# Two layers of a transformer block on one core: the shared expert cut as 384 + 320 units, with the last 64 of up and of gate in one tile

## The reference

```python
x = x + xattn(layernorm(x), ctx)            # 4 x 512 tokens, width 512, context width 256
h = rmsnorm(layernorm(x)); x2 = layernorm(x) + attention(h)      # 16 heads of 128, causal
t = rmsnorm(x2).reshape(2048, 512)
probs = softmax(t @ gate_w.T)               # 16 experts, the 6 best of each token, shares scaled to 1
routed = sum over the six: share * (silu(t @ eg.T) * (t @ eu.T)) @ ed.T      # 352 units an expert
shared = (silu(t @ sg_w.T) * (t @ su_w.T)) @ sd_w.T                          # 704 units, all 2048 tokens
out = x + x2 + routed + shared
```

## Time and profile before

| what | value |
|---|---|
| median of three runs | 2272.8 us |
| the profiled execution | 2274.86 us |
| its span, first to last instruction | 2273.0 us |
| mean granted TensorE clock | 0.979 |
| TensorE matmul busy | 2154.1 us, 95% |
| VectorE, ScalarE, GpSimd busy | 51%, 31%, 43% |
| `shared_expert`, first to last matmul | 1243.7 to 1482 us |

### The profile page before, as it was taken

One profiled execution on the slowest core, in us unless ns is written; L12 is line 12 of the kernel. 1 busy time (PEld: TensorE's weight loads), 2 busy tenths in 40 slices (PEclk: granted clock), 3 DMA queues, 4 the chain that ended last, 5 costly groups with the idle time before them and its releaser, 6 DMA issues. The chain is left out here.

```text
span 2273.0 us, 39678 instructions
## 1 busy us (share of the span) xinstructions
PE 2154.1 (95%) x11914; PEld 1870.6 (82%) x11915; DVE 1159.6 (51%) x2531; ACT 710.2 (31%) x1831; POOL 966.3 (43%) x1025
## 2 busy tenths in 40 slices
PE   6879999999999999999996999979999999999997
PEld 5668888989888898888875767779999999999996
DVE  5745646464655646465666576623333333333342
ACT  5633434343433434343434111012222222222221
POOL 1225454553645454553605035424444444444443
PEclk9989999999999999999998999989999999999998
DMA  3113344343434344343416111076776676667443
GB/s 134 61 47 112 126 153 138 123 172 120 139 124 152 112 159 154 111 168 114 158 38 245 43 65 46 33 248 157 189 196 156 179 200 162 157 182 201 83 78 56
DMA packets 139827, 300.64 MB, mean 132 GB/s; under 512 B 16704, under 2 KB 16704, under 8 KB 137472
## 3 DMA queue, kind: packets, MB, share of 16 engines
q1 hardware_dynamic: 114528, 241.25, 30.1%
q0 software_dynamic: 24960, 58.21, 13.5%
q10 hardware_dynamic: 288, 0.53, 0.1%
HBM read 177.51 MB, written 122.42 MB: 132 GB/s over the span
## 5 line engine op out<-in xcount | busy, mean ns | idle before, releaser
L567 POOL TENSOR_TENSOR chunk_hi<-chunk_raw,zero 128x512 fp32r<-128x512 f32 x153 | 159.3, 1041 | 242.2 <-DMA chunk_raw<-in_whole 242.2
L1575 DVE TENSOR_TENSOR prod<-ps,silu 128x352 f32<-128x352 f32 x111 | 58.2, 525 | 313.2 <-PE ps L62 274.4
L569 POOL TENSOR_TENSOR chunk_raw<-chunk_raw,chunk_hi 128x512 fp32r<-128x512 f32 x153 | 197.7, 1292 | 12.0
L785 DVE TENSOR_TENSOR pT_lo<-ps,pT_hi 128x384 fp32r<-128x384 f32 (+2 forms) x256 | 111.1, 455 | 176.5 <-ACT pT_hi L726 172.6
L1425 POOL DMA_INDIRECT out<-y,sidx x111 | 176.6, 1591 | 55.9 <-issue 35.1
L1432 POOL TENSOR_TENSOR carry<-ident 128x1 f32<-128x1 f32 x218 | 41.1, 188 | 327.1 <-DVE gidx L1572 256.7
L757 DVE SCALAR_TENSOR_TENSOR HS<-ps,rinv,HS 128x512 f32<-128x512 f32 x260 | 176.6, 738 | 2.8 <-PE ps L62 2.8
L715 ACT ACTIVATE prob<-ps,negmax 128x512 f32<-128x512 f32 (+3 forms) x256 | 131.6, 527 | 110.0 <-DVE negmax L746 110.0
L60 PE MATMUL ps<-wv_or_qk_hi,hT_hi 128*128 128x256 f32 x512 | 146.2, 286 | 8.3 <-POOL wv_or_qk_lo L562 8.3
L60 PE MATMUL ps<-ring,xT_0hi 128*128 x448 | 150.5, 336 | 1.7 <-DMA ring<-split_weights 1.7
L60 PE MATMUL ps<-ring,hT_hi 128*128 x333 | 140.8, 423 | 10.7 <-issue 9.0
(11 more groups left out here) (298 smaller groups left out, 6100.2 us busy)
## 6 DMA issues: line engine op xcount, KB each, us to landing
ring<-split_weights SPq DMA_DIRECT2D x240, 272.0 KB
chunk_raw<-in_whole SPq DMA_DIRECT2D x153, 256.0 KB, 2.6
split_weights<-chunk_hi SPq DMA_DIRECT2D x153, 256.0 KB, 2.4
split_weights<-chunk_raw SPq DMA_DIRECT2D x153, 256.0 KB, 2.6
xg<-in_wqk SPq DMA_DIRECT2D x16, 512.0 KB, 3.6
x<-in_x SPq DMA_DIRECT2D x4, 1024.0 KB, 5.6
xg<-in_wv SPq DMA_DIRECT2D x8, 512.0 KB, 4.0
x_spill<-x SPq DMA_DIRECT2D x4, 1024.0 KB, 3.9
```

The costliest lines, as they stand in the source:

```text
L567: nc.gpsimd.tensor_tensor(chunk_hi[k][:], chunk_raw[k][:], zero[:].to_broadcast([P, CH]), ALU.add).then_inc(chunk_high, 1)
L569: nc.gpsimd.tensor_tensor(chunk_raw[k][:].bitcast(F32R), chunk_raw[k][:], chunk_hi[k][:].bitcast(F32), ALU.subtract).then_inc(chunk_low, 1)
L785: nc.vector.tensor_tensor(pT[1][:, 0:split, w], ps_t[k % 2][:, 0:split * P].rearrange("p (j t) -> p j t", t=P), pT[0][:, 0:split, w].bitca ...
```

## The change

The 704 units are cut as 384 + 320. The first half has three full chunks of 128. The second has two full chunks and one last tile: in its 128 weight columns stand the last 64 units of up (columns 0 to 63) and the last 64 of gate (columns 64 to 127). So its 12 matmuls give up in partitions 0 to 63 and gate in 64 to 127 of one bank of `ps_u`. ScalarE takes silu of partitions 64 to 127 and writes it to partitions 0 to 63. In n = 4 to 7 the silu of the last chunk waits for pe_u, since there is no gate bank for it.

For down, that chunk's high part lies in partitions 0 to 63 and its low part in partitions 64 to 127 of one tile, and the high part of the down weights lies there twice. One matmul over 128 partitions gives high by high and low by high together; a second over 64 partitions gives high by low. So the chunk takes two matmuls a tile and not three.

The host lays the weights out to match; `warm` is loaded with 3072 columns a part instead of 2816, `wgu_1` with 2560 instead of 2816. The size of all of them together and of the space they lie in is unchanged, and so are all steps n = 0 to 3 but for the width of their third chunk (128 units instead of 96). The table work and its slots are unchanged.

```diff
+SHARED = [3 * P, 2 * P]
+REST = NSH * I - sum(SHARED)
+SGU = [2 * DC * SHARED[0], 2 * DC * SHARED[1] + DC * P]
+SAT = [0, SGU[0] + DN]
-WARM = EW + GU
+WARM = EW + SGU[0]
...
             for half in range(2):
-                sp.dma_start(warm[:, half * EW:half * EW + GU].bitcast(F32), split_w[half][:, 0:GU]).then_inc(ld_w, 16)
+                sp.dma_start(warm[:, half * EW:half * EW + SGU[0]].bitcast(F32), split_w[half][:, 0:SGU[0]]).then_inc(ld_w, 16)
...
+        w_rest = [w[:, 2 * DC * SHARED[1]:SGU[1]].rearrange("p (c i) -> p c i", c=DC) for w in wgu_1]
+        rest = lambda n, c: n >= NBLK and c == NI - 1
...
-                    for c, (_, w) in enumerate(IT):
-                        last = matmul3(nc, ps_d[i % 2][:], [h[0:w, c, i * P:(i + 1) * P] for h in hh[n % 2]],
-                                       [x[0:w, c, :] for x in wdn_s], c == 0, c == NI - 1)
+                    for c in range(NI):
+                        h_hi, h_lo = [h[:, c, i * P:(i + 1) * P] for h in hh[n % 2]]
+                        w_hi, w_lo = [x[:, c, :] for x in wdn_s]
+                        if rest(n, c):
+                            nc.tensor.matmul(ps_d[i % 2][:], h_hi, w_hi, start=False, stop=False)
+                            last = nc.tensor.matmul(ps_d[i % 2][:], h_hi[0:REST], w_lo[0:REST], start=False, stop=True)
+                        else:
+                            last = matmul3(nc, ps_d[i % 2][:], (h_hi, h_lo), (w_hi, w_lo), c == 0, c == NI - 1)
...
+                    if rest(n, c):
+                        for j in range(DC):
+                            h_hi, h_lo = [h[:, j, blk * S:(blk + 1) * S] for h in hT]
+                            w_hi, w_lo = [x[:, j, :] for x in w_rest]
+                            bank = ps_u[q % 2]
+                            nc.tensor.matmul(bank[:], w_hi, h_hi, start=j == 0, stop=False)
+                            nc.tensor.matmul(bank[:], w_hi, h_lo, start=False, stop=False)
+                            last = nc.tensor.matmul(bank[:], w_lo, h_hi, start=False, stop=j == DC - 1)
+                        last.then_inc(pe_u, 1)
+                        into_table(n, c)
+                        continue
...
-                    act.wait_ge(pe_g, q + 1)
+                    if rest(n, c):
+                        act.wait_ge(pe_u, q + 1)
+                    else:
+                        act.wait_ge(pe_g, q + 1 - max(0, n - NBLK))
...
-                    nc.scalar.activation(silu[0:w, :], ps_g[q % 2][0:w, :], ACT.Silu).then_inc(act_s, 1)
+                    if rest(n, c):
+                        nc.scalar.activation(silu[0:REST, :], ps_u[q % 2][REST:P, :], ACT.Silu).then_inc(act_s, 1)
+                    else:
+                        nc.scalar.activation(silu[:], ps_g[q % 2][:], ACT.Silu).then_inc(act_s, 1)
...
-                    nc.vector.tensor_tensor(hh[n % 2][1][0:w, c, :], prod[0:w, :],
-                                            hh[n % 2][0][0:w, c, :].bitcast(F32), ALU.subtract).then_inc(dve_h, 1)
+                    low = hh[n % 2][0][REST:P, c, :] if rest(n, c) else hh[n % 2][1][:, c, :]
+                    nc.vector.tensor_tensor(low, prod[0:w, :], hh[n % 2][0][0:w, c, :].bitcast(F32), ALU.subtract).then_inc(dve_h, 1)
```

More of the change, by code:

```diff
@@ L43 @@
 EW = GU + DN
-WARM = EW + GU
+SGU = [2 * DC * SHARED[0], 2 * DC * SHARED[1] + DC * P]
+SAT = [0, SGU[0] + DN]
+WARM = EW + SGU[0]
+assert SAT[1] + SGU[1] + DN == NSH * EW and WARM + 2 * SGU[1] <= EW + 3 * GU
 SLOTS = 3
@@ L990, in shared_expert @@
         at = placing(nc, slab + 4 * WARM)
-        gate_up = lambda w: w.rearrange("p (m c i) -> p m c i", m=2, c=DC)
-        wgu_1 = [at(f"wgu_1{s}", [P, GU], F32R) for s in ("hi", "lo")]
-        wgu_s = [[gate_up(warm[:, half * EW:half * EW + GU]) for half in range(2)], [gate_up(w[:]) for w in wgu_1]]
+        gate_up = lambda w, k: w[:, 0:2 * DC * SHARED[k]].rearrange("p (m c i) -> p m c i", m=2, c=DC)
+        wgu_1 = [at(f"wgu_1{s}", [P, SGU[1]], F32R) for s in ("hi", "lo")]
+        wgu_s = [[gate_up(warm[:, half * EW:half * EW + SGU[0]], 0) for half in range(2)], [gate_up(w[:], 1) for w in wgu_1]]
+        w_rest = [w[:, 2 * DC * SHARED[1]:SGU[1]].rearrange("p (c i) -> p c i", c=DC) for w in wgu_1]
+        rest = lambda n, c: n >= NBLK and c == NI - 1
         wdn_s = [sb(f"wdn_{s}", [P, NI, D], F32R) for s in ("hi", "lo")]
@@ L1053, in load_down @@
                     sp.dma_start(wdn_s[half][:].rearrange("p c n -> p (c n)").bitcast(F32),
-                                 split_w[half][:, k * EW + GU:(k + 1) * EW]).then_inc(ld_dn, 16)
+                                 split_w[half][:, SAT[k] + SGU[k]:SAT[k] + SGU[k] + DN]).then_inc(ld_dn, 16)
             def load_ring(half, columns):
@@ L1062, in _ @@
             for half in range(2):
-                sp.dma_start(wgu_1[half][:].bitcast(F32), split_w[half][:, EW:EW + GU]).then_inc(ld_gu, 16)
+                sp.dma_start(wgu_1[half][:].bitcast(F32), split_w[half][:, SAT[1]:SAT[1] + SGU[1]]).then_inc(ld_gu, 16)
             sp.wait_ge(pe_u, NI * NBLK)
@@ L1144, in _ @@
                     pe.wait_ge(ld_gu, 32)
-                for c, (i0, w) in enumerate(IT):
+                for c in range(NI):
                     q = NI * n + c
@@ L1148, in _ @@
                         pe.wait_ge(dve_p, q - 1)
+                    if rest(n, c):
[9 more added lines that the diff above has]
+                        continue
+                    i0 = c * P
                     for m, bank in enumerate((ps_g[q % 2], ps_u[q % 2])):
                         for j in range(DC):
-                            last = matmul3(nc, bank[0:w, :], [x[:, m, j, i0:i0 + w] for x in wgu_s[k]],
+                            last = matmul3(nc, bank[:], [x[:, m, j, i0:i0 + P] for x in wgu_s[k]],
                                            [h[:, j, blk * S:(blk + 1) * S] for h in hT], j == 0, j == DC - 1)
@@ L1310, in _ @@
             for n in range(STEPS):
-                for c, (_, w) in enumerate(IT):
+                for c in range(NI):
+                    w = REST if rest(n, c) else P
                     q = NI * n + c
@@ L1660 @@
     whole = np.concatenate([gu, down.reshape(NE, len(IT), P, D).transpose(2, 0, 1, 3).reshape(P, NE, DN)], axis=2)
-    whole = np.concatenate([whole[:, E:NE], whole[:, 0:E]], axis=1).reshape(P, NE * EW)
+    sg, su = (chunks(w(k).T) for k in ("sg_w", "su_w"))
+    sd = w("sd_w").T
+    half = lambda lo, hi: [m[:, :, lo:hi].reshape(P, -1) for m in (sg, su)]
+    rows_of = lambda lo, hi: chunks(sd[lo:hi]).reshape(P, -1)
+    ends = slice(NSH * I - REST, NSH * I)
+    shared = np.concatenate([*half(0, SHARED[0]), rows_of(0, SHARED[0]), *half(SHARED[0], sum(SHARED)),
+                             np.concatenate([su[:, :, ends], sg[:, :, ends]], axis=2).reshape(P, -1),
+                             rows_of(SHARED[0], sum(SHARED)), np.concatenate([sd[ends], sd[ends]])], axis=1)
+    whole = np.concatenate([shared, whole[:, 0:E].reshape(P, E * EW)], axis=1)
     whole = np.concatenate([whole, np.zeros((P, (CHUNKS + 2) * CH - NE * EW), np.float32)], axis=1)
```

10 lines of the change are left out of this document (6 added, 4 removed).

## The result

The changed kernel takes 2263.7 us (median of six runs, 2261.79 to 2265.53), the kernel before 2272.61 (six runs, 2270.62 to 2276.34). The ratio is 0.996 with a 95% interval of 0.9947 to 0.9973, so 8.9 us less, the interval 6 to 12. The profiled execution has a span of 2261.8 us against 2273.0.

What follows compares the result with a forecast made beforehand. TensorE's matmuls bound the kernel (95% busy), except short slots, paced by the table makers' round trip. Merged chunks 8.56 us plus slot (7, 6) 0.23 gave 8.8 off at the DMA queue: median 2272.8 to 2264.0 us, range 2259 to 2268.5.

Steps and rivals of the forecast that it cites:

- The pace of the short slots: Down's slots ending with a table: GpSimd's round trip sets the period, 3.23 to 3.26 us; one matmul less wins nothing.
- The naive 14.8 us: Steps 4 to 7: 64 matmuls less at 0.232 us, if nothing else sets the pace; as a rival 8%.
- The merged chunk: Last chunk of steps 4 to 7: 12 matmuls less gain 2.14 us a step, 8.56 in four, not 2.78 a step.
- silu for the most part: Steps 4 to 7: most of the 0.64 us lost a step is silu without its cover, the rest in_column.
- "0.232 us each, whatever the width", and steps 0 to 3 at nothing: Gate and up matmuls start 0.232 us apart at any width; a third chunk of 128 units in steps 0 to 3 costs nothing.
- The matmul over 64 partitions at 0.232: Down, steps 4 to 7: priced like 96 and 128 partitions; slot (7, 6) gains 0.23 us, down(7) 0.93.
- The drain rival: Down: the 64-partition matmul and the next wait for an empty array, 0.16 us each, twice a slot; 2264.6 us; 15%.
- The DMA queue sets the stage's end: Stage's end: a backlog from the third block's store ends the stage 8.8 us earlier; without backlog 9.7.
- the sign given for it: Stage's end: last add to the padding's landing takes longer than before by up to 0.9 us.
- Loads ahead of the stage: Before the stage: `warm` grows by 0.26 MB, 0.6 us; the norm behind it lands later but is covered, costing nothing.
- The slower rival: Steps 4 to 7: TensorE's idling lowers the granted clock to 1.2 GHz, matmuls 0.43 us apart, up to 2312 us; 5%.
- Given back in GpSimd: Shorter slots: three in_lane go from 2.45 to 3.88 us beside VectorE; all gains 2.1, 2270.7 us; rival, 12%.

Runs made afterwards that it cites:

- e2: The changed kernel with down's second product over all 128 partitions and issued twice, so nine matmuls a tile again: 2263.02 us, one run.
- e8: Against e6, the same 32 table batches spread over the step, after gate, after up and after two tiles of down: 2244.15 us, ratio 0.9869.
- e1: The changed kernel with the second product of down's last chunk over all 128 partitions instead of 64: 2262.81 us, ratio 0.9946.
- e10: The kernel before, nothing merged, with its table batches spread after gate and up of each chunk and once in down: 2259.06 us, ratio 0.993.
- e3: The changed kernel with the merged chunk's silu reading the gate bank of the chunk before, waiting for nothing new: 2258.91 us, one run.
- e4: The kernel before with only the shared expert's gate and up weights laid out chunk by chunk: 2269.73 us against 2275.26, ratio 0.9979.
- e7: Against e1, the third block of finished rows stored in four tiles, each after its own add: 2263.44 us, ratio 0.9957.
- e9: Against e8, the third block stored in tiles and the ring's remaining load issued before them: 2242.22 us, ratio 0.9864.
- e6: Against e1, the merged chunk as first instead of last in steps 4 to 7: 2260.84 us, ratio 0.9946.

## Why the prediction was right, point by point

The forecast of 2264.0 us came out at 2263.7, inside 2259 to 2268.5, and faster. The main mechanism was right and was shown, but that the medians agree to 0.3 us is in part luck: the interval of the difference is 6 to 12 us, and the profiled stage became 9.67 us shorter, not 8.8. Two terms were wrong. At TensorE's end they went against each other; at the stage's end only the first counts, since the queue begins to fill before most of the second.

- **The pace of the short slots**: right. Periods in down 3.23 to 3.26 us, unchanged (e2), and gone when the tables are moved (e8). The wait there is 0.44 us and not the 0.64 laid out; the 64-partition matmul has used up the difference (e1 has 0.65). The naive 14.8 us would have been the change's worth only with the tables elsewhere (e10).
- **The merged chunk**: 4.17 us was laid out for the first period, 4.18 measured; 3.86 for the second, 3.92 measured. The sum of 2.14 us a step was 2.07 (10.17 less 8.10). What was said of its parts was wrong: not silu for the most part, but silu and in_column side by side, with 0.13 us for silu alone (e3).
- **"0.232 us each, whatever the width", and steps 0 to 3 at nothing**: wrong on the gain's side. The distance went from 0.232 to 0.227 in the chunks not merged, a layout effect (e4): slot (5, 1) took 5.98 us instead of 6.10 and (5, 0) 6.10 instead of 6.22. The six such slots from (5, 0) to (7, 1) give 0.7 us, and table (4, 1) came 0.39 us earlier after the stage's start; but the time up to it differs by 0.7 us between two profiles of the same changed kernel (113.47 and 112.77), so that part is within its own spread.
- **The matmul over 64 partitions at 0.232**: wrong on the other side. The drain rival, given 15%, had the mechanism right. It put 0.16 us on each side, 0.32 a tile; measured are 0.09 before it, 0.20 after it and 0.10 one matmul later, 0.39. In the slots with a table it is hidden; in slot (7, 6) and in down(7) it took more than the 0.23 that a matmul less should give: from table (7, 5) to the last add the changed kernel needs 11.74 us, the kernel before 11.13. So TensorE's and VectorE's end came 8.68 us earlier after the stage's start (229.63 against 238.31), not 9.72.
- **The DMA queue sets the stage's end**: right, shown by e1, where TensorE ended 1.85 us earlier and the stage did not. But the sign given for it did not come: the way from the last add to the next stage was to grow by up to 0.9 us, and it shrank from 5.43 to 4.44, since the add came later and the queue earlier than laid out. The queue began to fill 9.30 us earlier (out stored at 1464.44 and 1474.50, less the stages' starts), not 8.79, and the stage ended 9.67 earlier, not 8.8. The 9.67 add up from the merged chunks' 8.2, the layout's 0.7, the 0.39 up to table (4, 1) and 0.37 in the queue behind the store. Tiles alone took 0.76 us off the way from the last add to the next stage (e7 against e1), tiles and an earlier load of the ring 2.05 (e9 against e8).
- **Loads ahead of the stage**: the norm of the third group started at 1216.98 after 0.21 us of idle, and ScalarE's copies of it at 1225.72, 8.7 us later (8.2 before). The norm was not late, and it was covered, as said.
- **The clock**: 1.00 throughout steps 4 to 7. The slower rival did not come.
- **Given back in GpSimd**: three in_lane took 2.01 to 2.45 us before and 2.01 to 2.32 after. It did not come either.

The Trainium skill (TensorEngine Tiling (Array Packing), Key Properties) says that changing the tiling mode drains TensorE. The trace of the changed kernel agrees: 0.32 and 0.43 us around the 64-partition matmul and 0.33 behind them, where 0.23 stands in e1.

## What to carry to other kernels

Before pricing matmuls taken away, look at what ends the wait behind them: with a second work woven in at fixed places, its round trip (here 3.26 us) is a floor for each slot. The same work at evenly spaced places took 17 us off the stage of the changed kernel (e6 to e8) and 15 off that of the kernel before (e10), where the arithmetic saved had given 9.7. Where two late inputs meet, price the step without each of them in turn; what each "costs" is not a share of the whole. And a product over half of the partitions among products over all of them was not cheaper but dearer (e1): fill the other half with something harmless, if the operands stand there anyway.

## What the runs showed of the hardware that was not expected

- A matmul over 64 partitions among matmuls over 128 costs 0.39 us more than its own 0.23: 0.09 before it, with its weight load late by 0.35, 0.20 after it and 0.10 one matmul later. 96 partitions among 128 cost nothing (0.23).
- The same matmuls, counts and shapes come 0.227 or 0.232 us apart by the place of their weight tiles in SBUF: 5.98 against 6.10 us for 24 and a table (e4). In rows of 352 columns they were slower than in tiles of 128 one behind the other, or in rows of 384 and 256.
